# Messages into 16 of 125 places summed from rows gathered per edge, 109 places left a dense product

## What is computed

```python
m = (embedding @ W_msg.T + b_msg).reshape(n, 4, 128)    # a message for each node and edge type
q = m[src, etype]                                       # one row of 128 for each edge
r = segment_sum(q, dst, num_segments=n)                 # summed at the edge's target
gi = r @ w_ih.T + b_ih;  gh = embedding @ w_hh.T + b_hh # then a GRU cell:
r_, z = sigmoid(i_r + h_r), sigmoid(i_z + h_z)
n_ = tanh(i_n + r_ * h_n);  embedding = (1 - z) * n_ + z * embedding
```

## Time and profile before

| | |
|---|---|
| median of 3 runs | 2418.93 us (2417.05 to 2979.36) |
| the profiled execution | 2416.61 us, span 2415.0 us, mean granted clock 0.927 |
| PE busy | 2159.3 us (89%) |
| DVE busy | 1384.7 us (57%) |
| ACT busy | 505.5 us (21%) |
| POOL busy | 235.7 us (10%) |
| the chain that ended last | PE 77%, DVE 9%, ACT 7% |
| of it PE L819, the dense sum | 43% |
| of it PE L898, the hops | 26% |

### The profile page before, as it was taken

The page is one execution under the profiler, slowest core; times in us unless marked ns, Lnnn a source line. Parts: engine busy times, 40 slices in busy tenths (PEclk is TensorE's granted clock), DMA queues, the critical chain, the costliest instruction groups (busy, mean ns, idle before and its releaser), DMA issues.

```text
span 2415.0 us, 40583 instructions
## 1 busy us (share of the span) xinstructions
PE 2159.3 (89%) x14377; PEld 1405.2 (58%) x14888; DVE 1384.7 (57%) x2714; ACT 505.5 (21%) x1122; POOL 235.7 (10%) x517
## 2 busy tenths in 40 slices
PE   4545555699999999999999999999999999999998
PEld 3223223599998989889544565444654446544465
DVE  8878778787777767787822347223463224542243
ACT  4877778400000000000300103000031000210010
POOL 4645555000000000000000000000000000000000
PEclk9565655699999999999999999999999999999999
DMA  2000000100000000005100000000000000010000
GB/s 77 22 33 22 22 33 22 50 2 1 2 2 2 2 2 1 2 1 151 47 1 1 1 1 1 1 1 1 1 1 1 1 1 1 1 27 1 1 1 28
DMA packets 23056, 34.26 MB, mean 14 GB/s; under 512 B 2573, under 2 KB 18939, under 8 KB 22466
## 3 DMA queue, kind: packets, MB, share of 16 engines
q1 hardware_dynamic: 19897, 30.56, 3.8%
q10 hardware_dynamic: 2944, 0.93, 0.2%
HBM read 18.04 MB, written 13.45 MB: 13 GB/s over the span
## 4 chain that ended last, share of the span: by engine, by line
PE 77%; DVE 9%; ACT 7%; issue 4%; ACTq 1%; DVEq 1%; POOL 0%; POOLq 0%; DMA 0%
PE ps L819 43%; PE ps L898 26%; PE ps L802 4%; ACT weighed L538 3%; PE ps L786 2%; ACT packed L531 2%; ACT words L520 1%; ACTq L511 1%; DVE marks L1093 1%; DVE dig L1121 1%; DVE big L1123 1%; PE ps L748 1%; DVEq L1080 1%; PE ps L883 1%; PE ps L704 1%
## 5 line engine op out<-in xcount | busy, mean ns | idle before, releaser
L819 PE MATMUL ps<-slots,m_parts 125*128 125x500 fp8e4 (+1 forms) x5600 | 1083.3, 353 | 1.5 <-DVE slots L1398 1.0
L819 PEld LDWEIGHTS ps<-slots,m_parts 125*128 125x128 f16 x5600 | 546.4, 98 | 487.5
L898 PE MATMUL ps<-parts,big 125*128 125x256 f16 x6125 | 669.5, 273 | 6.2 <-DVEq L1469 6.2
L898 PEld LDWEIGHTS ps<-parts,big 125*128 125x128 fp8e4 x6125 | 591.3, 98 | 63.5
L1398 DVE TENSOR_SCALAR slots<-big 128x3200 int32<-128x3200 int32 (+1 forms) x112 | 244.2, 2183 | 281.7 <-PE ps L819 281.6
L704 PE MATMUL ps<-hot_pair,weighed 125*128 125x228 f16 x1000 | 210.4, 359 | 180.8 <-ACT weighed L538 96.5
L704 PEld LDWEIGHTS ps<-hot_pair,weighed 125*128 125x128 f16 x1000 | 113.3, 120 | 277.9 <-ACT weighed L538 240.1
L538 ACT ACTIVATE weighed<-marks,win_w 125x128 f16<-125x128 f16 x625 | 195.6, 389 | 90.0 <-DVE marks L1093 89.0
L1526 DVE SCALAR_TENSOR_TENSOR r_parts<-ps,over,r_parts 128x500 f16<-128x500 f32 (+1 forms) x28 | 19.1, 684 | 229.7 <-ACT r_parts L615 229.7
L1533 DVE SCALAR_TENSOR_TENSOR gate_r<-ps,over,gate_r 128x500 f32<-128x500 f32 (+1 forms) x28 | 19.1, 681 | 226.6 <-PE ps L802 226.6
L477 ACT ACTIVATE rs<-rs 125x25 f32<-125x25 f32 (+3 forms) x5 | 1.1, 216 | 703.0 <-DVE rs L971 703.0
(11 more groups left out here) (204 smaller groups left out, 1328.8 us busy)
## 6 DMA issues: line engine op xcount, KB each, us to landing
packed_counts<-packed SPq DMA_DIRECT2D x16, 625.0 KB, 2.9
big<-packed_counts SPq DMA_DIRECT2D x4, 1600.0 KB, 7.6
big<-packed_counts SPq DMA_DIRECT2D x3, 1200.0 KB, 6.4
hd<-in_x SPq DMA_DIRECT2D x1, 1562.5 KB
x_again<-in_x SPq DMA_DIRECT2D x1, 1562.5 KB
big<-x_after_hops SPq DMA_DIRECT2D x1, 1400.0 KB
x_after_hops<-x SPq DMA_DIRECT2D x4, 224.0 KB
out<-big SPq DMA_DIRECT2D x4, 224.0 KB
```

The costliest lines, as they stand in the source:

```text
L819: last = pe.matmul(ps[:, k % 2, 0:SIZES[k] * Q], m_parts[0:Q, a, h, t * F:(t + 1) * F], slots_f8[0:Q, t % 2, 0:SIZES[k], a, 0:Q], start=a ...
L898: last = pe.matmul(ps[:, n % RING, 0:2 * F], tot_f8[0:Q, c, a, :], both((parts0, parts1)[par], a), start=a == 0, stop=a == TILES - 1)
```

## The change

The packed counts keep only the first 112 places of each tile (`QS`, 14 blocks of 8), and the dense product goes over 109 of them (`QD`): 436 or 327 columns for 500 or 375. The other 16 places x 25 tiles = 400 targets are summed edge by edge:

- After a step's messages are made, SP writes `m_parts` to `m_dram` (five pieces of 5 tiles, 6.4 MB in all), one row of 512 B (both halves) for each node and type.
- The 16 places are 8 pairs. The edges of a pair lie in a window of at most 15 chunks of 125 edges (`GW`; in these inputs the eight windows are 14 or 15 chunks). For each chunk POOL issues one indirect DMA that gathers 125 rows: 120 in a step, in 24 lots of 5, into four shelves of 5 rows (`picked`).
- TensorE multiplies each gathered chunk and half (stationary, 125 x 128) with a one-hot matrix of 50 targets (moving, `hot_to`), 240 products of 50 columns in a step, ten to a lot, put between the dense products by `LOTS_AT`. The 400 sums stay in bank 6 until a turn of their own, `("picked", 0)`, ahead of the last dense block, does their gates.
- New tables for this are made in the front: on POOL the edge's row number (4 x source + type) and its target as f32, on TensorE two more sets of 11 transposes, on ACT two more pairs of casts, behind the windows a loop over the 8 pairs on POOL, and on DVE 8 one-hot operations (`mark_targets`) in the ninth hop.
- A window of over 15 chunks sends the kernel to its general path.

```diff
+QD = 109
+NBD = (QD + BQ - 1) // BQ
+QS = NBD * BQ
+TILE_D = TILES * QS
+GW = 15
+PC = 2 * TILES
+PAIRS = (Q - QD) // 2
+ORDER = [("dense", 0), ("dense", 1), ("dense", 2), ("dense", 3), ("dense", 4), ("dense", 5), ("picked", 0), ("dense", 6)]
+TURNS = len(ORDER)
+TURN_OF = {what: u for u, what in enumerate(ORDER)}
+LOT = 5
+LOTS = PAIRS * GW // LOT
+SHELVES = 4
+USES = LOTS // SHELVES
+LOTS_AT = {(1, 0): (0, 1), (1, 1): (2,), (1, 2): (3,), (1, 3): (4, 5), (2, 0): (6,), (2, 1): (7,), (2, 2): (8, 9), (2, 3): (10,),
+           (3, 0): (11, 12), (3, 1): (13,), (3, 2): (14,), (3, 3): (15,), (4, 0): (16, 17), (4, 1): (18,), (4, 3): (19, 20),
+           (5, 0): (21,), (5, 1): (22,), (5, 2): (23,)}
+RING_AT = (TILES * TILE_D + 63) // 64 * 64
+STORED = [(0, 5), (5, 10), (10, 15), (15, 20), (20, 25)]
...
-        big1 = sb("big1", [128, BIG], U8)
+        big_room = sb("big1", [128, RING_AT + SHELVES * LOT * 4 * F], U8)
+        big1 = big_room[:, 0:BIG]
+        picked = big_room[:, RING_AT:].bitcast(F16).rearrange("p (r w h f) -> p r w h f", r=SHELVES, w=LOT, h=2)
...
-            m_parts = sb("m_parts", [128, TILES, 2, TYPES * F], F16, b)
-            slots = sb("slots", [128, 2, 4 * TILES * 128], U8, b)
+            m_parts = sb("m_parts", [128, TILES, TYPES, 2, F], F16, b)
+            slots = sb("slots", [128, 2, 4 * TILE_D], U8, b)
+            hot_to = sb("hot_to", [128, PAIRS, GW, PC], U8, b)
+            edge_row = sb("edge_row", [128, PAIRS * GW], I32, b)
+            iota_to = sb("iota_to", [128, PC], F32, b)
+            win_to = sb("win_to", [128, PAIRS * GW], F32, b)
...
+        def turn_places(what, i):
+            if what == "dense":
+                return slice(START[i], START[i] + SIZES[i]), slice(0, QD)
+            return slice(0, TILES), slice(QD, Q)
+
+        def turn_size(what, i):
+            return SIZES[i] * QD if what == "dense" else TILES * (Q - QD)
+
+        def picked_sums(i):
+            return ps[:, 6, 0:turn_size("picked", i)].rearrange("p (q c) -> p c q", c=TILES)
+
+        def picked_parts(i, u, h):
+            return r_parts[:, u % 2, h, 0:turn_size("picked", i)].rearrange("p (c q) -> p c q", c=TILES)
...
-                    a, z = START[k] * TILE_BYTES, (START[k] + SIZES[k]) * TILE_BYTES
-                    sp.dma_start(big1[:, a:z].rearrange("p (b n) -> p b n", b=NB),
-                                 packed_dram[:, :, START[k] * TILES * BQ:(START[k] + SIZES[k]) * TILES * BQ]).then_inc(s_pblk[k], 16)
+                    a, z = START[k] * TILE_D, (START[k] + SIZES[k]) * TILE_D
+                    sp.dma_start(big1[:, a:z].rearrange("p (b n) -> p b n", b=NBD),
+                                 packed_dram[:, 0:NBD, START[k] * TILES * BQ:(START[k] + SIZES[k]) * TILES * BQ]).then_inc(s_pblk[k], 16)
                     store_x2(k)
-                sp.wait_ge(s_slot, TYPES * (BLOCKS * (STEPS - 1) + 1))
+                with sp.Fori(0, STEPS) as s:
+                    for first, last in STORED:
+                        sp.wait_ge(s_mp, TILES * s + last + 1)
+                        for lo, hi in ((0, ROWS_A), (ROWS_A, Q)):
+                            sp.dma_start(m_dram.rearrange("(p a t) f -> p a (t f)", a=TILES, t=TYPES)[lo:hi, first:last, :],
+                                         m_parts[lo:hi, first:last, :, :, :].rearrange("p a t h f -> p a (t h f)")).then_inc(s_mst, 16)
+                sp.wait_ge(s_slot, TYPES * (BLOCKS * (STEPS - 1) + 2))
...
+            pool.wait_ge(s_edges[1], 16)
+            pool.wait_ge(s_edges[2], 16)
+            pool.tensor_scalar(edge_g[0:ROWS, 0, :], edge_i[0:ROWS, 1, :], float(TYPES), None, ALU.mult).then_inc(s_grow4, 1)
+            pool.tensor_copy(edge_g[0:ROWS, 1, :], edge_i[0:ROWS, 2, :]).then_inc(s_grow4, 1)
+            pool.wait_ge(s_grow4, 2)
+            pool.tensor_tensor(edge_g[0:ROWS, 0, :], edge_g[0:ROWS, 0, :], edge_g[0:ROWS, 1, :], ALU.add).then_inc(s_grow, 1)
+            pool.wait_ge(s_grow, 1)
+            pool.wait_ge(s_edges[0], 16)
+            pool.tensor_copy(edge_g[0:ROWS, 1, :], edge_i[0:ROWS, 0, :]).then_inc(s_grow, 1)
+            pool.memset(edge_kind[:, NCH:PAD], 0)
+            pool.memset(edge_to[:, NCH:PAD], NOWHERE)
+            pool.iota(iota_to[:, :], [[1, PC]], base=0, channel_multiplier=0, allow_small_or_imprecise_dtypes=True)
+            pool.iota(pair_off[:, :], [[PC, PAIRS]], base=TILES * QD, channel_multiplier=0, allow_small_or_imprecise_dtypes=True)
...
+            pool.wait_ge(s_gtab, 2)
+            pool.wait_ge(s_pair, 1)
+            for pair in range(PAIRS):
+                lo = pool.value_load(pair_lo[0:1, pair:pair + 1], min_val=0, max_val=NCH)
+                pool.tensor_copy(edge_row[0:CH, pair * GW:(pair + 1) * GW], edge_kind[0:CH, ds(lo, GW)])
+                pool.tensor_tensor(win_to[0:CH, pair * GW:(pair + 1) * GW], edge_to[0:CH, ds(lo, GW)],
+                                   pair_off[0:CH, pair:pair + 1].broadcast_to([CH, GW]), ALU.subtract).then_inc(s_to, 1)
...
+                for s in range(STEPS):
+                    pool.wait_ge(s_mst, 16 * 2 * len(STORED) * (s + 1))
+                    for lot in range(LOTS):
+                        r = lot % SHELVES
+                        pool.wait_ge(s_got_used[r], USES * s + lot // SHELVES + 1)
+                        for w in range(LOT):
+                            at = lot * LOT + w
+                            pool.indirect_dma_start(
+                                out=picked[0:CH, r, w, :, :].rearrange("p h f -> p (h f)"), out_offset=None, in_=m_dram[:, :],
+                                in_offset=bass.IndirectOffsetOnAxis(ap=edge_row[0:CH, at:at + 1], axis=0)).then_inc(s_got[r], 16)
...
+            cast(tab[0:CH, 0, 0:NCH], 0).then_inc(s_tabs, 1)
+            act.wait_ge(s_gtr, 1)
+            cast(edge_kind[0:CH, 0:NCH], 6).then_inc(s_gtab, 1)
+            act.wait_ge(s_tr, 3)
+            cast(tab[0:CH, 1, 0:NCH], 4).then_inc(s_tabs, 1)
...
+            act.wait_ge(s_gtr, 2)
+            cast(edge_to[0:CH, 0:NCH], 2).then_inc(s_gtab, 1)
...
+                    if u + 1 < TURNS and ORDER[u + 1][0] == "picked":
+                        act.wait_ge(s_got_used[SHELVES - 1], USES * s + USES + 1)
+                        sum_high(picked_sums(0), picked_parts(0, u + 1, 0))
...
+                whole = max(TURN_OF["picked", 0], TURN_OF["dense", BLOCK_OF[a]])
+                pe.wait_ge(s_el, TURNS * s + whole + 1 - (TURNS - BLOCKS))
...
-                        last = pe.matmul(ps[:, k % 2, 0:SIZES[k] * Q], m_parts[0:Q, a, h, t * F:(t + 1) * F],
-                                         slots_f8[0:Q, t % 2, 0:SIZES[k], a, 0:Q],
+                        last = pe.matmul(ps[:, k % 2, 0:SIZES[k] * QD], m_parts[0:Q, a, t, h, :],
+                                         slots_f8[0:Q, t % 2, 0:SIZES[k], a, 0:QD],
...
+            def picked_rows(s, lot):
+
+                r, (pair, first) = lot % SHELVES, divmod(lot * LOT, GW)
+                wait_alone(s_got[r], 16 * LOT * (USES * s + lot // SHELVES + 1))
+                for w in range(LOT):
+                    for h in range(2):
+                        last = pe.matmul(ps[:, 6, pair * PC:(pair + 1) * PC], picked[0:CH, r, w, h, :], hot_to_f8[0:CH, pair, first + w, :],
+                                         start=first + w == 0 and h == 0, stop=first + w == GW - 1 and h == 1, skip_group_check=True)
+                last.then_inc(s_got_used[r], 1)
...
-                            block_gates(k - 1)
-                        if t == 1 and k == BLOCKS - 1 and not more_steps:
-                            for done in range(3):
-                                pe.wait_ge(s_emb, BLOCKS * STEPS + done + 1)
-                                out_transposes(done)
-
+                            turn_gates("dense", k - 1)
+                        if t == 1 and k and ORDER[TURN_OF["dense", k] - 1][0] == "picked":
+                            turn_gates(*ORDER[TURN_OF["dense", k] - 1])
+                        for lot in LOTS_AT.get((k, t), ()):
+                            picked_rows(s, lot)
+                        if t == 2 and k == BLOCKS - 1 and not more_steps:
+                            pe.wait_ge(s_emb, BLOCKS + TURNS * STEPS - 1)
+                            for tiles in range(3):
+                                out_transposes(tiles)
...
-                n = SIZES[k % BLOCKS] * TILE_BYTES // 4
-                first = START[k % BLOCKS] * TILE_BYTES
+                n = SIZES[k % BLOCKS] * TILE_D // 4
+                first = START[k % BLOCKS] * TILE_D
...
+            def mark_targets(pair):
+
+                at = win_to[0:CH, pair * GW:(pair + 1) * GW]
+                TT(hot_to[0:CH, pair, :, :], iota_to[0:CH, :].rearrange("p (o n) -> p o n", o=1).broadcast_to([CH, GW, PC]),
+                   at.rearrange("p (m o) -> p m o", o=1).broadcast_to([CH, GW, PC]), ALU.is_equal).then_inc(s_sel, 1)
...
+                        if scales_at and c >= TILES - PAIRS:
```

(15 more changed lines are left out.)

231 lines of the change are left out of this document (132 added, 99 removed).

## The result

The changed kernel takes 2348.63 us (median of 4, 2346.54 to 2350.52) against 2419.47 for the kernel before on the same chip (4 runs): a ratio of 0.971, 95% interval 0.9691 to 0.9729. Forecast were 2345 us. One of the four executions before (2979 us), and one of a variant further down (3655 us), fell into a slower state, and the ratios leave them out. The profiled execution took 2346.54 us with a span of 2345.0, where the one before had 2415.0.

A forecast was written before the change was run, and what follows sets the result against it. TensorE's streaming was taken to bound the four steps, over half of the span. 2416.6 - 4 x (33.8 - 12.2) + 13 = 2343.2 us, so 2345 for the median; own range 2319 to 2362, stated range 2317 to 2480.

The forecast's parts named there:

- The narrower product: Dense products of 436 and 327 columns cost 186.3 and 139.5 ns, in proportion to columns: 33.8 us less a step.
- The gates: Gate products on TensorE: 3125 columns in total before and after, in one turn more, so no change.
- DVE's 1.41 us a tile: Block 0's message phase: DVE becomes the bound at 1.41 us a tile, so only 1.9 us comes back there.
- The picked products: 240 products of 50 columns a step at 48.2 ns each, 11.6 us; with each lot's wait 12.2 us a step.
- Rival 2: Picked pairs cost 98 ns (2393 us), or g is near 1.8 (2409 us): within 2% of before; 20% chance.
- The waits for rows: TensorE stopped by late gathered rows: no stall taken; nothing lost while g is under 1.67 us.
- g: Time from one gather to the next on POOL; taken as 1.12 us, plus at most 65 us over 120 gathers.
- POOL waiting for shelves: Expected in the new profile: POOL, up to four lots ahead, waits for free shelves, not TensorE for rows.
- Rival 1: POOL's gathers bind: g = 2.0 gives 329 us a step and 2505 us in all, slower; 22% chance.
- Once only: Costs outside the repeated steps: front 6 us, ninth hop 4.5, first messages 1.5, output transposes 1; sum 13 us.
- the upper variant of the forecast: Front: up to 12 us later if POOL and DVE exclude each other; floor 1 us, 6 taken.
- Ninth hop: Seven mark operations on DVE ahead of the last tile, 5.7 us, about 1.2 in slack: next hop 4.5 us late.

## Why the prediction was right

The time, 2345 for 2348.6, and the step, 289.1 for 288.5 us, were right, in part by luck: four terms were off, and the errors nearly cancel. In a step the narrower product gave about 2 us less, the picked products cost about 5 us less, and waits forecast as none took 2.3 us; what is paid once cost 6 us more. Together that is 4 us late, and the profiled execution was 3.3 us late (2346.5 for 2343.2).

- **The narrower product**: forecast -33.8 us a step, measured -30.9, with about 0.9 us of picked products and lone loads still in it, so some -31.8 as an estimate. A product of 327 columns took 140.4 to 140.8 ns and not 139.5, one of 436 columns 187.0 and not 186.3, together 1.1 us. The gates, forecast as nothing, took 0.4 us more: in the chain their runs of 18 products are four of 3.34, two of 2.52 and one of 3.25 us, before four of 3.80 and two of 2.87 (one more of 2.52 and of 2.87 lies in the message phase). For the last 0.5 us I have no row. That DVE's 1.41 us a tile sets the pace of the message phase held: block 0 from the first message behind the pause to its gates went from 68.4 to 63.3 us, 5.1 as forecast.
- **The picked products**: forecast +12.2, measured +6.5 for 232 of the 240; with the other 8 and the lone loads some 7.4 as an estimate. The term was mis-sized at "laid end to end": 26.9 ns for the pair and 21.3 ns for its columns. The row of ten in 0.25 us shows 25 ns a product, no more than the pair with one column in the earlier trace rows. So the 50 columns are not paid on top of the weight load; that they run while the next weights are loaded fits this, but whether the load or some other limit of TensorE sets the 25 ns, no run here tells. Rival 2 (98 ns) is out. The Trainium skill's figure for a pair, about 81 ns ("TensorE: Matmul & The Clock Gate", section "Back-to-back issue gap"), is one for 128 columns; with 50, no run here had such a floor.
- **The waits for rows**: forecast 0, measured 2.3 us a step. g was taken at 1.12 us plus up to 0.5, so at most 1.62; it was 1.52 plus 0.13 = 1.643. The form of the sum held (89 + 120 g against 90.5 + 120 g), but its limit did not: 1.67 was the g at which it reaches a stream of 289.1 us, and the stream was 286.3. With that and 90.5 the edge is at 1.63 us, and the kernel stands 0.01 us past it. So of the 2.3 us, 1.4 are the gathers' total (287.7 for 286.3) and 0.8 are lots placed by hand that came late singly. "POOL waiting for shelves" was wrong: it never did.
- **Rival 1** was nearer than its 22% sounds. The kernel is just past the edge, and nine pairs are far over it: 313 us a step, 2450 us. The mechanism named for it was right: the fast unpack stops a gather. The Trainium skill says so of a DVE instruction that uses both ports ("SBUF — State Buffer", section "Who interferes with whom"). The estimate of 25 us a step made by it was nearly twice the measured 13.9: only 12 fast unpacks meet gathers, and each costs 1.16 us, not 1.6. What kept the sign is that the other 108 gathers pay 1.5 to 1.9 us and nearly all of them 1.5, not the 2.0 of rival 1. Had the 8 slow unpacks beside gathers stretched one each too, a step would have grown by some 9 us as an estimate, less than the 22 us that the change gains.
- **Once only**: forecast 13 us, measured about 19 (four steps shorter by 22.2 make 88.8, the span is shorter by 70.0). Front: TensorE's 625 one-column products start at 449.17 for 439.98, 9.2 us, forecast 6. It was the upper variant of the forecast, but not by the path it named: POOL's constants at 28.8 us were in time for DVE at 34.6, and it was DVE itself that was stretched by 7.4 us. Ninth hop: from its start (1016.03, after 1025.13) to the end of the tenth (1153.4, after 1169.4) it was 137.4 us before and 144.3 after, 6.9 more for a forecast of 4.5. The forecast had the waits right and lacked the slower products behind them. TensorE in time order in the first tile of the tenth hop and behind it, and the stretch there (busy by engine, then granted clock, DMA share, GB/s):

```profile
1098.52 0.28 PE L1034 MATMUL ps<-parts,big 125*128 125x256 f16 x1 [1.68 <-DVE parts L1459]
1101.56 67.83 PE L1034 MATMUL ps<-parts,big 125*128 125x256 f16 x601 [2.76 <-DVE parts L1459]
```

```profile
1100.00:1104.00 4.00, 2.44 (x12) 1.86 (x15) 3.56 (x10) 0.00 (x0) 0.00 (x0) 0.50 0.00 0
```

The two waits are 4.4 us. Behind them the clock was granted at 0.50, and the 601 products took 67.8 us; at full clock, as before (1025 of them in 112.07 us), they take 65.7. The remaining 3 us of the 19 lie between the hops and the first gates; they were not taken apart.

## What to carry to other kernels

Where work moves to an idle engine, write down both chains to the point where they meet, and ask how far apart they end, not only which is shorter: here they ended less than 2 us apart, the lateness came out singly at four places, and one pair more turned 3% of gain into 1% of loss. A chain that runs through an engine for 24% of the span says that it is close, not that removing it gives 24%; leaving its work out showed 0.4%. For the cost of many small instructions take the spacing in the chain, not the time of one in time order, and give it two prices, the longer of load and product alone and the sum of both: here the lower one, 25 ns, was the right one.
